# A graph network's first gather round: each group's count block one group later on PE and ACT, messages ahead of block one-hots on DVE

## What is computed

```
xw  = x @ W0                          # node features
ew  = edge_attr @ edge_w              # (100000, 16) @ (16, 128)
msg = xw[src] * ew                    # one row of 128 for each edge
out = segment_sum(msg, dst) + b0
x   = layernorm(x + out)
...
# second layer: ht[src, type] * edge_weight, segment_sum, relu, layernorm
# third layer: edge weights from a small MLP, normalised by degrees, layernorm
# fourth: four times  agg = segment_sum(x[src], dst); x = relu((x + agg) @ W1 + b1) @ W2 + b2
```

## Time and profile before

| what | us |
|---|---|
| median of 3 runs | 5869.15 (5864.26 to 5869.99) |
| the profiled execution, its own time | 5808.96 |
| its span, first to last instruction | 5807.0 |
| PE busy / DVE busy / POOL busy | 3565.6 / 2355.4 / 2476.6 |
| first round of gathers, first to last issue | 81.3 to 1585.4 |
| second round | 1664.4 to 2842.7 |

### The profile page before, as it was taken

How to read it: one execution, slowest core, us unless ns; L and a number is a source line. 1 busy time by engine, 2 the same in 40 slices (tenths; PEclk the granted TensorE clock), 3 DMA queues, 4 the chain that set the end, 5 groups by cost and what they waited for, 6 DMA issues and landing times. The chain is left out here.

```text
span 5807.0 us, 66376 instructions
## 1 busy us (share of the span) xinstructions
PE 3565.6 (61%) x22480; PEld 2267.2 (39%) x22480; DVE 2355.4 (41%) x5012; ACT 1317.1 (23%) x3052; POOL 2476.6 (43%) x2412
## 2 busy tenths in 40 slices
PE   3555656666655656666522222222677799999997
PEld 3333333333333434443322222222567455555554
DVE  6343433343434545455344444444577303121203
ACT  1111211212121222211133333333466201010101
POOL 3655444554546666666566666666311000000000
PEclk7778788788777878877755555555699899999998
DMA  2222222222222222222255555555667686767674
GB/s 84 75 69 92 81 77 90 81 81 90 81 85 75 91 83 87 84 88 87 80 150 159 162 159 162 161 163 160 214 231 247 234 309 228 301 241 301 239 302 168
DMA packets 509159, 863.93 MB, mean 149 GB/s; under 512 B 111675, under 2 KB 284775, under 8 KB 508868
## 3 DMA queue, kind: packets, MB, share of 16 engines
q1 hardware_dynamic: 345136, 545.24, 26.8%
q0 software_dynamic: 90496, 189.62, 11.8%
q10 hardware_dynamic: 73236, 125.49, 5.9%
HBM read 632.93 MB, written 227.18 MB: 148 GB/s over the span
## 5 line engine op out<-in xcount | busy, mean ns | idle before, releaser
L724 POOL DMA_INDIRECT big<-xw_rows,srci x784 | 784.0, 1000 | 790.8 <-DVE big L1882 494.6
L754 POOL DMA_INDIRECT big<-axt_rows,srci x784 | 802.4, 1023 | 436.2 <-issue 342.0
L1569 PE MATMUL psS<-big,xsb 128*128 128x448 f16 x2744 | 971.1, 354 | 16.2 <-issue 8.4
L1569 PE MATMUL psA<-big,xsb 128*128 128x448 f16 x2744 | 970.6, 354 | 0.0
L724 POOL DMA_INDIRECT big<-ht_rows,reli x784 | 780.7, 996 | 436.1 <-issue 230.2
L1350 PE MATMUL psA<-xsb 128*128 128x416 bf16 x1960 | 444.1, 385 | 530.0 <-ACT xsb L853 398.2
L1350 PE MATMUL ps<-xsb 128*128 128x416 bf16 x1960 | 486.4, 404 | 363.3 <-issue 187.8
L1449 PE MATMUL ps<-identh,xsb 128*128 128x128 bf16 x784 | 101.4, 310 | 676.5 <-DVE xsb L2055 497.6
L1324 PE MATMUL psS<-big 128*128 128x128 f32 x3136 | 444.0, 302 | 74.2 <-DMA big<-ht_rows,reli 66.2
L1824 DVE TENSOR_SCALAR xsb<-iotaS,keys 128x512 bf16<-128x512 f16 x980 | 285.4, 357 | 499.7 <-remote 183.2
L1350 PEld LDWEIGHTS psA<-xsb 128*128 128x128 bf16 x1960 | 202.5, 107 | 731.0 <-ACT xsb L853 424.6
(11 more groups left out here) (273 smaller groups left out, 4929.5 us busy)
## 6 DMA issues: line engine op xcount, KB each, us to landing
big<-A_rows SPq DMA_DIRECT2D x112, 2744.0 KB, 13.5
A_rows<-xsb ACTq DMA_DIRECT2D x196, 416.0 KB
xg_rows<-big SPq DMA_DIRECT2D x98, 512.0 KB
big<-xg_rows SPq DMA_DIRECT2D x98, 512.0 KB
marks_rows<-big SPq DMA_DIRECT2D x98, 354.0 KB
big<-marks_rows SPq DMA_DIRECT2D x98, 354.0 KB
big<-srcq_list SPq DMA_DIRECT2D x98, 256.0 KB
ht_rows<-big ACTq DMA_DIRECT2D x28, 512.0 KB
```

What stands on the lines that cost most here:

```text
L724: pool.indirect_dma_start(ring[g % len(ring)][:, j * D:(j + 1) * D], None, table[:, :], bass.IndirectOffsetOnAxis(ap=lists[:, g * TPG + j: ...
L754: pool.indirect_dma_start(wide[g % NS][:, j, :], None, axt_rows[:, :], bass.IndirectOffsetOnAxis(ap=srci[:, g * TPG + j:g * TPG + j + 1], ...
L1569: m = pe.matmul(sums, xs[:, t, k, :], Aring[:, r, :, t, :], start=(t == 0), stop=(t == NB - 1))
```

## The change

PE and ACT skip the count block at step 0, do block g-1 at step g, and the last block behind the loop. The wait ahead of turning the attributes asks for one block less. On DVE message g moves ahead of the block one-hots of g. SP's queue and POOL's are as they were. The form with several windows per group (`more > 0`) isn't taken with these inputs and isn't changed; `plain_groups` also serves the second round, where there are no messages and the moved lines do the same as before.

```
 # ACT
                 for g in range(NG):
                     if g + 2 < NG:
                         turned_attr(g % 2, g // 2 + 1)
-                    block_stage(g % 2, g // 2 + R1N, bank0)
+                    if g:
+                        block_stage(1 - g % 2, (g - 1) // 2 + R1N, bank0)
                     early_n1(g)
+                block_stage(1, NIT - 1 + R1N, bank0)
                 summed(R0)
 # PE
+            def banks_free_to(g):
+                pe.wait_ge(b_ev, max(g + 1, 0) * KS + 2)
...
                     if g + 2 < NG:
-                        banks_free(it, b)
+                        banks_free_to(g - 2)
                         turn_attr(b, it + 1)
                     window_sums([msg[:, 0, :], msg[:, 1, :]], b, it)
                     if g + 2 < NG:
                         pe.wait_ge(s_attrT[b], it + 2)
-                    block_counts(b, it + R1N, bank0)
+                    if g:
+                        block_counts(1 - b, (g - 1) // 2 + R1N, bank0)
                     early_n1(g)
+                block_counts(1, NIT - 1 + R1N, bank0)
                 whole_n1(NCH - 1)
 # DVE, plain_groups
                     make_onehots(b, bases[g], 0, it, it + R.w0, weights)
-                    if n0 is not None:
-                        block_onehots(b, it + n0)
                     if messages:
                         dve.wait_ge(r_land[g % NS], landed(R, 0, g))
                         dve.wait_ge(s_ew[b], it + 1)
                         dve.tensor_tensor(msg[:, b, :], slots[g % NS], ps4[:, 0:GE], ALU.mult).then_inc(s_msg[b], 1)
+                    if n0 is not None:
+                        block_onehots(b, it + n0)
                     if g:
                         finish(g - 1)
```

## The result

The changed kernel takes 5802.2 us in the median of 10 runs (5790.0 to 5842.6), the kernel before beside it on the same chip 5860.75 us (10 runs, 5834.88 to 5881.59): a ratio of 0.991, 95% interval 0.9884 to 0.9935. The point forecast was 5805. The profiled execution of the changed kernel has an own time of 5804.03 us and a span of 5801.6 us.

The account below looks back on a forecast made before the run. The prediction took a loop of waits through POOL, DVE and PE in the first gather round as the bound. Terms -52, -21, -13, +3.7 and +18 (clock) gave -64, so 5869 became 5805 us; range over all cases 5700 to 5965.

Parts of the forecast that it names:

- the rhythm of 8 gathers: First round, POOL: bursts of 8 gathers replace 16, so kept-back increments come after 10 + 3.1 us, not 20 + 3.1.
- the hold: First round: PE's increments seem not to reach others from about 8 us into POOL's gather burst until 3.1 us after.
- Plain groups: First round, 26 groups without relation products or norm steps: 15.1 to 13.1 us each, -52 us.
- relation groups: First round, 42 groups with relation products: 15.1 to 14.6 us each, -21 us.
- norm steps: First round, steps with norm work: message 2.6 us earlier, ten such pauses counted, half taken, -13 us.
- The new wait at the turn: PE's turn of edge attributes, behind SP's later load: 3.6 us, or 1.7 where relation products lie ahead.
- PE's loop: First round: PE's cycle through counts, store, attribute load, turn and sums, 11.7 us against 10.0 of POOL issue.
- The tail: End of the first round: the last block's counts no longer lie beside other work, +3.7 us.
- Rival D: First round: forecast's rhythm, but one-hots stretch gathers in 49 groups, 2.6 us each, 127 us; 5932 us, chance 0.04.
- A: First round slower: bursts of 16 stay, the store, SP and attribute-load loop costs; 5973 us, chance 0.35.
- C: First round much faster: single bursts bring it to the second round's 12.0 us a group; 5571 us, chance 0.08.
- B: First round: no change, PE's factors release message and POOL in both orders, gains and new wait cancel; 5869 us, chance 0.15.

Follow-up runs that it names:

- e7: Kernel before plus one wait: SP loads edge attributes only behind the store of block g, not g-1; chip with the hold: ratio 1.0016.
- e1: Kernel before with only the counts, their copy and store one group later, DVE's order as before; chip without the hold: ratio 1.0576.
- e3: Kernel before plus only the wait for the store of block g ahead of the attribute load; chip without the hold: ratio 1.0548.
- e11: Changed kernel plus four dependent GpSimd memsets after every four first-round gathers; chip without the hold: ratio 1.0563 against the kernel before, 5257.91 us.
- e12: Same edit as e1 on the kernel before (counts one group later, DVE's order as before), run again; chip without the hold: ratio 1.0571.
- e5: The changed kernel itself, run again beside the kernel before on a chip with the hold: ratio 0.9879.
- e8: Kernel before plus four dependent GpSimd memsets after every four first-round gathers; chip with the hold: 5612.11 us against 5874.87, ratio 0.9546.
- e10: Kernel before plus one small dependent GpSimd memset after every four first-round gathers; chip with the hold: ratio 0.9826.

## Why the prediction was right

The sign and the size came as forecast, and so did POOL's pause after every group. The sum that led there put the gain in the wrong places, and that its total came within 6 us (-64 against -58.5) is luck. First what it credited, then the terms.

- **What the sum credited to what.** It put DVE's new order down as a loss, 1.9 us after each hold, and the rhythm of 8 gathers as the gain. On chips with the hold the order alone gives 0.9931, the rhythm alone 1.0016, and the change without its new wait 0.9881. So this step of the forecast is wrong: the gain goes with the order, and it is there at either rhythm. How the order gains it is only in part known. Faster gathers are 16 of the 55 us; the rest is open, and so is what the later counts add.
- **The groups in the sum.** Plain groups were to gain 2.0 us each (-52), relation groups 0.5 (-21), norm steps 13 us in all. The twelve plain groups measured above gained nothing (182.5 and 183.1 us, against a forecast of -24), the first six steps of the rounds of 14 lost 5, and the last eight gained 68, 1.4 us a group. Errors of opposite sign stand behind the total.
- **Pauses after every group**: 86 instead of 46, half as long, as forecast. The median pause is near 4 us, and what ends each is DVE's message.
- **DVE after the counts.** Forecast from the counts' arrival to the start of the message: 4.6 us. Measured: 314.60 to 318.59, 4.0 us; the 0.45 for the load of the base isn't there. The order on DVE (block one-hots, add, one-hots, message) is the one that was worked out.
- **The new wait at the turn**, read off SP's queue: 369.3 us in 87 pieces, 4.2 us each, right behind SP's L514, where 3.6 and 1.7 were forecast. From the end of counts to the turn it is 313.56 to 320.28, 6.7 us instead of 6.1.
- **PE's loop was mis-sized: 11.7 us forecast, 14.0 measured** (14.4 from the turn at 305.89 to that at 320.28, 13.6 to the next at 333.92). Some 0.4 of the 2.3 us are in the load's path above (6.7 and 6.4 us for 6.1). The rest is mostly the clock. From turn to end of counts I took 5.6 us from rows at full clock (1.00 granted from 333.50 to 335.50); it took 7.7 us (305.89 to 313.56) and 7.3. PE had stood for 5 us before. The granted clock over the sums is 0.50 of full speed, the 1.2 GHz level, and they took 3.64 us instead of 1.95. My charge for the clock was 18 us in 26 groups. The sums cost 118 us more of PE's time, a few of them from two groups more in the window. First the kernel before, then after, from 90 to 1600 us; last, the stretch of the sums:

```profile
L1324 PE MATMUL psS<-big 128*128 128x128 f32 x1536 | 191.6, 279 | 0.0
```

```profile
L1326 PE MATMUL psS<-big 128*128 128x128 f32 x1568 | 309.6, 380 | 0.0
```

```profile
306.20:309.40 3.20, 3.20 (x17) 3.20 (x17) 0.00 (x0) 0.27 (x1) 2.59 (x3) 0.50 0.19 49
```

- **The hold after short bursts** was carried over from long ones. At the add of the sums it is gone: 0.9 us of waiting in the whole stage, where I had forecast pieces of 5 us. Part of it moved to the block one-hots (190.4 us for a releaser not found, up to 14.8 us at a time; 72.0 before).
- **The tail**: +3.7 forecast. From the end of the last gather of the round to the first of the second it was 78 us before and 74 after, so the tail doesn't show the cost.
- **The rule on the shared port.** The trace of before showed block one-hots that stretch no gather, and I gave it nothing. That reading holds for block one-hots and messages: in the changed kernel 68 gathers start under L1831, the longest 1.07 us. It does not hold for the one-hots at L1790 (L1797 after): 63 gathers start under them in before, 1.30 us each in the mean, and 11 in after. The Trainium skill (SBUF — State Buffer, "Reading the diagram") gives the lock against GpSimd to DVE instructions in a two-port mode and also to those with two SBUF inputs, the latter only against a GpSimd operation that reads SBUF; I had used the first case alone. The trace agrees with the second as far as it goes: L1797 has both inputs in SBUF (`big<-big,dstf`) and stretches gathers in the changed kernel to up to 1.99 us, the message has one in PSUM (`big<-big,ps`) and stretches none. Rival D had the sign wrong: the change takes away overlap that costs, 16 us of it.
- **Rivals.** A (bursts of 16 stay) and C (12.0 us a group) did not happen. B's result, no change, is what e7 gave.

The range held the result. The forecast is for chips with the hold; by e1, e3, e11 and e12 the change should be some 5 to 6% slower on one without it. That is an estimate: the changed kernel itself was not run on such a chip.

## What to carry to other kernels

When an increment seems late by many microseconds while another engine issues gathers back to back, test the issue itself with a short pause before rearranging the work: here idle memsets gained 4.5%, the reordering 0.9% (1.2% in e5). The new wait inside the change cost 5.5% where there was no hold, so run such a kernel on several chips before believing a per cent. When a total comes true, look where in the stage it was won. And cost matmuls that come right behind a new wait at the clock that rows show after a stand, not at the clock of the rows where they now are.

## What the hardware showed that was not expected

- Two kinds of chips, or of states that last: the same kernel takes 4974 to 4980 us on two chips and 5838 to 5875 us on at least three. In the second round, the same 784 gathers take 1021 to 1029 us from first to last issue (10.4 to 10.5 us a group) on the one and 1178 to 1226 us on the other. What makes the difference is open.
- On the slower kind, what PE and ACT finish reaches waiting engines late while gathers are issued at 1.25 us steps: 14.4 us in the case of PE's sums that end at 312.35 and are added at 326.79. A pause of 1.3 to 1.5 us after every four gathers ends it (e8), one of 0.5 us only in part (e10).
- A gather that starts under DVE's f32 one-hots of 128x1024 takes 1.84 us in the mean of e12's 96 and 1.30 in the mean of before's 63, instead of 0.94; those under block one-hots or a message take 0.94 to 0.98 in the mean.
